# First-layer projections as two 64-row products side by side, and two groups of heads in one attention accumulator

## Chip, core and metric

One core of one Trainium2 chip runs the whole kernel in one launch. The metric is the device time of that core in microseconds (us); lower is better. Engines: PE is TensorE's matrix product and PEld its weight load, DVE is VectorE, ACT is ScalarE, POOL is GpSimd, and SP starts the DMAs.

## What is computed

Two layers work on 16 batches of 512 tokens with 128 features, all in float32. Both have 16 heads of 8 features.

```python
# layer 0, attention (b=16, t=512, H=16, HD=8)
q_c = xh @ W_DQ.T @ W_UQ.T;  q_c_norm = rms_norm(q_c);  q_r = q_c_norm @ W_QR.T
k_c, v_c = split(xh @ W_DKV.T @ W_UKV.T);  k_r = xh @ W_KR.T
scores = concat(q_c_norm, q_r) @ concat(rms_norm(k_c), k_r).T * HD ** -0.5   # causal
out = softmax(scores) @ v_c @ W_O.T
# layer 0, beside it: r * (relu(xk @ W_k.T) ** 2 @ W_v.T), x mixed with the token before
# layer 1, attention: softmax(q @ k.T * scale + phi_bias) @ v, then w_proj and b_proj
# layer 1, beside it: gelu(x @ W1) @ W2, W1 and W2 composed from 32 primitives
```

The weights of layer 0's attention are folded at the start into one matrix `wcat` (128 rows, four blocks of 128 columns: q, k, the second part of k, and the values). As every head uses the same 8x8 map, each block is block-diagonal: it is zero outside its 8x8 blocks, and so also outside the two 64x64 quarters on its diagonal.

## The kernel before

**Bodies and slots.** The work of one batch in one layer is spread over "bodies" of 64 slots, four quarters u = 0 to 3 of 16 slots each. Body n does the attention of batch n (offset 0), prepares batches n+1 and n+2, and finishes batch n-1. In quarter u it computes, for the four heads of group u, the transposed scores (`scores_t`, L643) and, two quarters ahead, the scores once more in the other layout for their row maxima (`scores_max`, L664 and L668, with the causal mask added by products at L680). The two kinds use opposite 64-row halves of the array, so they stand next to each other in the order. ACT exponentiates the transposed scores into `probs` (L937), DVE reduces the maxima (L1144 to L1175), POOL zeroes the causal triangle (`mask`, L1283) or multiplies by the near bias (L1309), and PE multiplies `probs` by the values (`pv`, L627) one quarter later. Each layer has two preparing bodies, sixteen with attention and a finishing one; the last three of layer 0 overlap the first three of layer 1, so 14 attention bodies of layer 0 and 15 of layer 1 run alone.

**Order of the other work.** The tables `WORK_USES` and `OTHER_WORK` (L113 to L129) give for each piece the slot and the batch offset. Each engine walks the slots in order and does what is due (`other`), so an engine that waits for one piece holds back all that stands behind it. The names used below are: OT0 to OT3 (transposes of the accumulator of a group), MT0 to MT3 (transposes of the maxima), XT (transposes of the normalised input), PJ0 to PJ3 (projections of one block of 128 tokens each), QT and KT (queries and keys), FR, FK and FV (the work beside attention), MIX, LN, NORM, SQUARE, MEAN, ROOT and SCALE_QK (steps of DVE and ACT), POST (the two sums of the residual on POOL) and STORE (four indirect DMAs of POOL, L1231).

**PSUM.** Three banks form the ring `scores_transposed`, taken by ACT. Four banks form the ring `scores_for_max`, taken mostly by DVE (`BY_DVE`, L124). A piece claims the next bank of its ring and so waits until the piece three or four claims earlier is read. The eighth bank is `pv_acc`.

**The accumulator.** A group has four heads. Head j of the group writes rows 32j to 32j+31 of `pv_acc`: 8 value sums, the sum of probabilities (a column of ones in `vals`) and 23 rows of zeros. When the four `pv` steps of a group are done, ACT copies the bank to `accS` (L926, at slot 12 of the next quarter), PE transposes it in four products (L693), and DVE takes the reciprocal of the sums (L1045) and multiplies (L1050) into `att`. This is done four times for a batch. In layer 0, POST waits for OT1's result, since it is the last part of `att` of batch n-1.

**The projections.** PJt multiplies 128 tokens (stationary, 128 rows by 128 columns) by the whole of `wcat` (moving, 512 columns), L721, into one bank of `scores_transposed`, and ACT copies it to `big` (L857).

```python
mm(work, xnT[:, B.parity(2), 1 + P * t:1 + P * t + P],
   wcat[:].rearrange("p a n -> p (a n)"), start=True, stop=True)
```

## Time and profile before

| | us |
|---|---|
| median of 3 runs | 1824.24 (1821.36 to 1831.1) |
| the profiled execution's own time | 1823.52 |
| its span, first to last instruction | 1821.7 |
| PE busy | 1622.6 (89%) |
| DVE busy | 1469.0 (81%) |
| ACT busy | 1322.1 (73%) |
| POOL busy | 942.4 (52%) |

The span is the stretch that the trace covers; 1.8 us lie around it. Busy shares are means over stages with different limits. Lines are those of the kernel before. A float32 product is recorded twice (two records of a product and two of its weight load), a float32 transpose once.

### The profile page before, as it was taken

What the parts mean: (1) busy time and instruction counts of PE and PEld (TensorE: products, weight loads), DVE (VectorE), ACT (ScalarE), POOL (GpSimd) and SP (SyncE); (2) the same over time, 40 slices, a digit from 0 to 9 for tenths busy, and PEclk for the clock granted to TensorE, in tenths of its full rate; (3) what the DMA queues carried; (4) which work ended last, traced back from release to release, by engine and by line L of the source; (5) the groups of instructions that cost most, each with busy time, mean ns of one, the idle gap of its engine ahead of it and who ended that gap; (6) DMA issues with size and microseconds to landing.
All of it is one profiled execution on the core that took longest, in us unless ns stands there. A gap on an engine that the chain in (4) does not pass through costs nothing.

```text
span 1821.7 us, 33616 instructions
## 1 busy us (share of the span) xinstructions
PE 1622.6 (89%) x11850; PEld 640.0 (35%) x11850; DVE 1469.0 (81%) x2653; ACT 1322.1 (73%) x2566; POOL 942.4 (52%) x1144
## 2 busy tenths in 40 slices
PE   4798898888889888889999999999999999999995
PEld 2453343333333333333332333323333233333331
DVE  4358878888888788888879888998889888898881
ACT  1227777776777677677778888888888788888875
POOL 2124555555555555455455556655565555564555
PEclk9759999999999999999999999999999999999999
DMA  8312323232322323323222322232222321222200
GB/s 269 58 40 61 68 63 65 62 66 62 71 71 70 67 71 63 71 74 72 59 53 59 59 58 52 46 70 59 58 52 45 71 58 54 48 54 62 61 14 18
DMA packets 133126, 116.41 MB, mean 64 GB/s; under 512 B 16856, under 2 KB 125664, under 8 KB 132960
## 3 DMA queue, kind: packets, MB, share of 16 engines
q1 hardware_dynamic: 126272, 100.64, 24.7%
q0 software_dynamic: 4096, 8.40, 1.4%
q10 hardware_dynamic: 2592, 5.24, 0.9%
q8 instruction: 95, 1.56, 0.4%
q14 instruction: 71, 0.58, 0.1%
HBM read 79.63 MB, written 33.55 MB: 62 GB/s over the span
## 4 chain that ended last, share of the span: by engine, by line
PE 46%; DVE 22%; ACT 10%; issue 7%; POOL 7%; DMA 5%; SPq 2%; DVEq 0%; POOLq 0%; ACTq 0%
PE pv_acc L627 14%; PE scores_transposed L643 10%; ACT probs L937 6%; DVE maxs L1144 4%; PE scores_transposed L771 4%; DMA stacks<-parts_scratch 4%; PE scores_for_max L664 3%; DVE maxs L1147 3%; DVE xn L1067 2%; DVE maxs L1175 2%; POOL x_between_layers L1231 2%; PE scores_transposed L743 2%; PE scores_for_max L779 2%; SPq L478 2%; PE scores_for_max L693 1%
## 5 line engine op out<-in xcount | busy, mean ns | idle before, releaser
L937 ACT ACTIVATE probs<-scores_transposed 128x512 f32<-128x512 f32 x1664 | 919.3, 601 | 214.4 <-PE scores_transposed L643 206.8
L643 PE MATMUL scores_transposed<-stacks 62*128 62x512 bf16 (+3 forms) x2048 | 581.4, 347 | 50.6 <-ACT probs L937 34.4
L1309 POOL TENSOR_TENSOR probs<-probs,near_bias 128x512 f32<-128x512 f32 x256 | 325.1, 1274 | 370.1 <-ACT probs L937 369.8
L627 PE MATMUL pv_acc<-probs,vals 128*32 128x512 f32 (+3 forms) x4096 | 474.8, 536 | 7.8 <-POOL probs L1283 3.8
L1144 DVE TENSOR_REDUCE maxs<-scores_for_max 128x2 f32<-128x1024 f32 x322 | 388.1, 1220 | 78.1 <-PE scores_for_max L664 76.8
L643 PEld LDWEIGHTS scores_transposed<-stacks 62*128 62x128 bf16 x2048 | 153.6, 94 | 618.5 <-ACT probs L937 303.8
L664 PE MATMUL scores_for_max<-stacks 60*128 60x512 bf16 x1024 | 336.3, 385 | 18.1 <-DVE maxs L1144 8.7
L1147 DVE TENSOR_REDUCE maxs<-scores_for_max 128x1 f32<-128x512 f32 x380 | 250.6, 682 | 25.7 <-PE scores_for_max L664 22.6
L668 PE MATMUL scores_for_max<-stacks 60*128 60x512 bf16 (+3 forms) x1024 | 255.1, 315 | 9.8 <-DMA stacks<-parts_scratch 8.0
L1283 POOL TENSOR_SCALAR_AFFINE_SELECT probs<-probs 128x512 f32<-128x512 f32 x256 | 175.4, 700 | 151.1 <-ACT probs L937 150.9
L1175 DVE TENSOR_REDUCE maxs<-scores_for_max 128x1 f32<-128x512 f32 x256 | 174.9, 683 | 90.3 <-PE scores_for_max L680 86.3
L680 PE MATMUL scores_for_max<-causal_halves,ident_halves 64*128 64x128 bf16 (+2 forms) x1280 | 188.6, 235 | 0.0
L1171 DVE TENSOR_REDUCE maxs<-scores_for_max 128x1 f32<-128x384 f32 x256 | 140.3, 548 | 59.0 <-PE scores_for_max L680 58.5
L627 PEld LDWEIGHTS pv_acc<-probs,vals 128*32 128x32 f32 x4096 | 82.4, 109 | 164.8 <-issue 129.3
L680 PEld LDWEIGHTS scores_for_max<-causal_halves,ident_halves 64*128 64x128 bf16 x1280 | 113.8, 99 | 35.8 <-issue 5.7
L1215 POOL TENSOR_TENSOR parts<-rest,parts 128x512 bf16<-128x512 f32 x64 | 75.5, 1180 | 61.0 <-ACT parts L914 61.0
L664 PEld LDWEIGHTS scores_for_max<-stacks 60*128 60x128 bf16 x1024 | 77.0, 93 | 51.2 <-DVE maxs L1144 27.8
L1166 DVE TENSOR_REDUCE maxs<-scores_for_max 128x2 f32<-128x512 f32 x128 | 87.5, 684 | 8.1 <-PE scores_for_max L680 7.0
L693 PE MATMUL scores_for_max<-ident,accS 128*128 128x128 f32 x512 | 85.6, 291 | 1.3 <-ACT accS L926 0.8
L926 ACT ACTIVATE accS<-pv_acc 128x512 f32<-128x512 f32 x128 | 77.3, 604 | 10.4 <-PE pv_acc L627 8.7
L668 PEld LDWEIGHTS scores_for_max<-stacks 60*128 60x128 bf16 x1024 | 76.8, 95 | 21.6 <-DMA stacks<-parts_scratch 8.2
L743 PE MATMUL scores_transposed<-xnT,w 128*128 128x512 f32 x128 | 72.8, 651 | 9.3 <-ACT probs L937 7.9
(129 smaller groups left out, 2093.1 us busy)
## 6 DMA issues: line engine op xcount, KB each, us to landing
stacks<-parts_scratch SPq DMA_DIRECT2D x768, 64.0 KB
parts_scratch<-parts SPq DMA_DIRECT2D x64, 384.0 KB, 2.6
x_tile<-in_L_attn_x_dram SPq DMA_DIRECT2D x16, 256.0 KB, 2.8
probs<-in_fc_B_dram ACTq DMA_DIRECT2D x1, 4096.0 KB, 19.3
stage_a<-in_fc_A_T_dram SPq DMA_DIRECT2D x1, 4096.0 KB, 16.9
stacks<-mT SPq DMA_DIRECT2D x256, 4.0 KB
x_res<-in_L_attn_x_dram SPq DMA_DIRECT2D x16, 256.0 KB, 3.6
x_tile<-x_between_layers SPq DMA_DIRECT2D x16, 256.0 KB
```

Of the source, the lines that this page charges most:

```text
L627: last = mm(acc[32 * j:32 * j + 32, q0:T], vals[:, B.parity(off), kt, G * pu + j, :], probs[:, row, column:column + width], start=(kt == 0 ...
L643: last = mm(st[:, bank, column:column + T - q0], ks[p][rows, h, P * kt:P * kt + P], qs[p][rows, h, q0:T], start=True, stop=True)
L664: mm(bank, qs[p][rows, h, P * qt:P * qt + P], ks[p][rows, h, :], start=True, stop=True).then_inc(s["s1_ready"], 1)
L668: mm(bank[:, column:column + P * (qt + 1)], qs[p][rows, h, P * qt:P * qt + P], ks[p][rows, h, 0:P * (qt + 1)], start=True, stop=False, ski ...
L680: last = mm(masked, ident_halves[half, n, :], mask, start=False, stop=(n == 1), skip_group_check=True)
L937: fn(probs[:, row, :], st[:, B.use(("st", u, number)).bank, :], ACT.Exp, scale=SCALE).then_inc(s["exp_done"], 1)
L1144: v.reduce_max(maxs[:, su % 2, :].rearrange("p (e x) -> p e x", e=E)[:, :, column], s1[:, bank - 1:bank + 1, :], AX_X).then_inc(s["red_don ...
L1147: v.reduce_max(maxs[:, su % 2, column:column + 1], s1[:, bank, :], AX_X).then_inc(s["red_done"], 1)
L1171: v.reduce_max(maxs[:, su % 2, wide:wide + 1], bank[:, 0:3 * P], AX_X)
L1175: v.reduce_max(maxs[:, su % 2, column:column + 1], bank, AX_X).then_inc(s["red_done"], 1)
L1283: g.affine_select(out=diag, in_=diag, compare_op=ALU.is_ge, fill=0.0, base=0, pattern=[[0, G], [1, P]], channel_multiplier=-1).then_inc(s[ ...
L1309: g.tensor_tensor(diag, diag, near_bias[:, kt, :].unsqueeze(1).broadcast_to([P, G, P]), ALU.mult).then_inc(s["emul_pool"], 1)
```

## The change

1. *Accumulator.* Groups 2m and 2m+1 share `pv_acc`: head j of the even group fills rows 32j to 32j+15, head j of the odd group rows 32j+16 to 32j+31. The stationary operand still has 32 columns; for an odd group it begins 16 columns earlier, in the zeros of the head before. The copy to `accS`, the four transposes and the reciprocal are done twice for a batch (OA, OB) and not four times. The reciprocal has 32 columns in place of 16. There are still four multiplications into `att`, now two behind each reciprocal.
2. *Projections.* PJ0 to PJ3 become PJ0 and PJ1. Each claims a bank in both rings and issues four products: for two blocks of tokens, the upper and the lower 64 rows by the 256 columns of `wcat` that are not zero for them. The two halves write different banks, and ACT reads both banks (the names PJ0b and PJ1b stand for the second ones).
3. *Slots.* Layer 0: MIX 0 to 2, FR 5 to 6, FK 8 to 9, XT 11 to 14, MT1 17 to 19, MT2 37 to 32; OT0 (9) and OT2 (40) go, OT1 (16) is OA, OT3 (49) is OB; PJ at 22, 24, 27, 31 becomes PJ at 24 and 31. Layer 1: NORM 16 to 18, OT0 (6) and OT2 (36) go, OT1 (20) is OA (19), OT3 (48) is OB, and AT, PR, VP and STORE move by one slot.

```diff
-VW = 32
+VW, PAIR = 32, 2
+NPAIR = NG // PAIR
+ACC = VW // PAIR
...
 WORK_USES = {
...
+    0: {"MT0": (2, 0, 0), "FR": (6, 0, 1), "FK": (9, 0, 1), "XT": (14, 0, 2), "FV": (15, 0, 1),
+        "OA": (16, 0, -1), "MT1": (19, 0, 0), "PJ0": (24, 0, 2), "PJ1": (31, 0, 2), "MT2": (32, 0, 0),
+        "FT": (35, 0, 1), "QT": (47, 1, 2), "OB": (49, 0, 0), "MT3": (54, 0, 1), "KT": (59, 1, 2)},
+    1: {"H0": (3, 0, 1), "MT0": (4, 0, 0), "H1": (9, 0, 1), "H2": (15, 0, 1), "MT1": (17, 0, 0),
+        "OA": (19, 0, -1), "XT": (21, 0, 2), "AT": (25, 0, -1), "H3": (28, 0, 1), "PR": (30, 0, -1),
...
+BY_DVE = ("OA", "OB", "FV", "QT", "KT", "PR")
+SECOND_HALF = {"PJ0": "PJ0b", "PJ1": "PJ1b"}
...
-    0: {"MIX": (0, 1), "LN": (3, 2), "NORM": (7, 2), "VALUES": (15, 1), "POST": (21, -1),
+    0: {"MIX": (2, 1), "LN": (3, 2), "NORM": (7, 2), "VALUES": (15, 1), "POST": (21, -1),
...
-    1: {"LN": (3, 2), "NORM": (16, 2), "BESIDE": (22, -1), "STORE": (33, -1)},
+    1: {"LN": (3, 2), "NORM": (18, 2), "BESIDE": (22, -1), "STORE": (34, -1)},
...
                     for j in range(G):
...
-                        last = mm(acc[32 * j:32 * j + 32, q0:T], vals[:, B.parity(off), kt, G * pu + j, :],
-                                  probs[:, row, column:column + width], start=(kt == 0), stop=(kt == NT - 1),
-                                  skip_group_check=True)
+                        first = VW * (G * pu + j) - ACC * (pu % PAIR)
+                        last = mm(acc[VW * j:VW * j + VW, q0:T], columns[:, first:first + VW],
+                                  probs[:, row, column:column + width], start=(kt == 0 and pu % PAIR == 0),
+                                  stop=(kt == NT - 1 and pu % PAIR == PAIR - 1), skip_group_check=True)
...
+                        for n, name in enumerate(SECOND_HALF):
+                            if B.due(name, slot):
+                                banks = claim(name), claim(SECOND_HALF[name])
+                                if n == 0:
                                     taken_out("XT")
+                                for t in range(2):
+                                    for e in range(E):
+                                        rows, tokens = slice(HALF * e, HALF * e + HALF), 1 + P * (2 * n + t)
+                                        last = mm(banks[e][:, 2 * P * t:2 * P * t + 2 * P]
+                                                  .rearrange("p (a n) -> p a n", a=4),
+                                                  xnT[rows, B.parity(2), tokens:tokens + P], wcat[rows, :, rows],
+                                                  start=True, stop=True)
+                                        if t == 1:
+                                            last.then_inc(full, 1)
...
+                                for e, half in enumerate((name, SECOND_HALF[name])):
+                                    work = filled(half).rearrange("p (t a n) -> p t a n", t=2, a=4)
...
+                                    fn(big[:, 2 * n:2 * n + 2, :].rearrange("p t (a n) -> p t a n", a=4)
+                                       [:, :, :, HALF * e:HALF * e + HALF], work, ACT.Copy).then_inc(taken, 1)
...
-                            if j == 0 and kt == NT - 1 and B.has(eo):
+                            if j == 0 and kt == NT - 1 and u % PAIR == 0 and B.has(eo):
...
+                            link(v.reciprocal(rsum[:], heads[:, :, HD]), "rec", NPAIR, pair + 1, oo)
...
+                            for n in range(PAIR):
+                                first = G * HD * (PAIR * pair + n)
+                                last = v.tensor_tensor(
...
-                            pool.wait_ge(s["dve_taken"], B.use("OT1").taken[1])
+                            pool.wait_ge(s["dve_taken"], B.use("OA").taken[1])
```

## Rows read from the trace of the kernel before

**Rows 1.** The page, part 1: busy time of each engine.
```profile
PE 1622.6 (89%) x11850; PEld 640.0 (35%) x11850; DVE 1469.0 (81%) x2653; ACT 1322.1 (73%) x2566; POOL 942.4 (52%) x1144
```

**Rows 2.** Windows, three layer-0 periods, slot 32 to 32: length, PE, PEld, DVE, ACT, POOL, clock, DMA.
```profile
487.35:535.82 48.47, 42.87 (x386) 18.71 (x386) 40.06 (x88) 34.76 (x66) 25.94 (x37) 0.96 0.24 67
535.82:583.76 47.94, 42.55 (x386) 18.64 (x386) 39.87 (x88) 34.87 (x66) 26.04 (x37) 0.96 0.25 68
583.76:633.43 49.67, 44.27 (x386) 18.75 (x386) 39.98 (x88) 34.87 (x66) 26.07 (x37) 0.93 0.30 66
```

**Rows 3.** Windows, layer 0: slots 32 to 47, 0 to 15, 16 to 31; next period's 48 to 63.
```profile
487.35:498.65 11.30, 9.37 (x101) 4.43 (x105) 9.61 (x19) 9.84 (x18) 3.72 (x7) 1.00 0.10 26
...
507.70:523.75 16.05, 13.07 (x100) 5.41 (x100) 15.19 (x38) 10.08 (x19) 6.95 (x11) 0.89 0.46 125
523.75:535.82 12.07, 11.87 (x98) 4.76 (x97) 7.93 (x17) 7.98 (x16) 9.12 (x12) 1.00 0.16 45
...
547.04:557.13 10.09, 9.82 (x94) 4.59 (x94) 7.41 (x16) 6.94 (x15) 6.21 (x9) 0.83 0.12 40
```

**Rows 4.** Timeline, start and length, layer 0 around slots 21 to 32, POOL and PE.
```profile
526.60 1.27 POOL L1249 TENSOR_TENSOR x_new<-x_res,att 128x512 f32<-128x512 f32 x1 [1.61 <-DVE att L1050]
...
535.12 0.65 POOL L1283 TENSOR_SCALAR_AFFINE_SELECT probs<-probs 128x512 f32<-128x512 f32 x1
...
535.82 1.06 PE L627 MATMUL pv_acc<-probs,vals 128*32 128x512 f32 x8 [0.21 <-POOL probs L1283]
...
583.76 0.64 PE L627 MATMUL pv_acc<-probs,vals 128*32 128x512 f32 x4 [0.21 <-POOL probs L1283]
```

**Rows 5.** Timeline, layer 0, slots 44 to 47, PE and DVE.
```profile
544.97 0.33 PE L643 MATMUL scores_transposed<-stacks 62*128 62x384 bf16 x1 [1.14 <-ACT probs L937]
544.98 0.33 PE L668 MATMUL scores_for_max<-stacks 60*128 60x384 bf16 x1
...
545.13 1.21 DVE L1096 TENSOR_TENSOR big<-big,rrms 128x1024 f32<-128x1024 f32 x1
...
546.49 0.63 PE L737 MATMUL scores_for_max<-ident,big 128*128 128x128 f32 x4 [0.47 <-DVE big L1096]
```

**Rows 6.** Timeline, layer 0, slots 7 to 11, PE and DVE.
```profile
516.44 0.66 PE L693 MATMUL scores_for_max<-ident,accS 128*128 128x128 f32 x4
...
516.90 2.50 DVE L1067 TENSOR_SCALAR xn<-x_tile,mv,rstd 128x128 f32<-128x128 f32 x4
...
519.55 0.80 PE L704 MATMUL scores_transposed<-ident,xn 128*128 128x128 f32 x4 [1.95 <-DVE xn L1067]
```

**Rows 7.** Groups by form, whole span: count, busy us, mean ns, idle before.
```profile
L721 PE MATMUL scores_transposed<-wcat,xnT 128*128 128x512 f32 x128 | 72.8, 653 | 0.7 <-ACT xnT L839 0.7
L627 PE MATMUL pv_acc<-probs,vals 128*32 128x256 f32 x512 | 41.8, 399 | 0.0
L693 PE MATMUL scores_for_max<-ident,accS 128*128 128x128 f32 x512 | 85.6, 291 | 1.3 <-ACT accS L926 0.8 <-DVE maxs L1147 0.5
L926 ACT ACTIVATE accS<-pv_acc 128x512 f32<-128x512 f32 x128 | 77.3, 604 | 10.4 <-PE pv_acc L627 8.7
L1045 DVE RECIPROCAL rsum<-scores_for_max 128x16 f32<-128x16 f32 x128 | 31.4, 245 | 23.6 <-PE scores_for_max L693 23.6
L1050 DVE TENSOR_TENSOR att<-scores_for_max,rsum 128x128 f32<-128x128 f32 x128 | 37.3, 291 | 4.4
L1092 DVE RECIPROCAL ssq<-ssq 128x128 f32<-128x128 f32 x16 | 15.2, 953 | 0.6
```

**Rows 8.** Windows, one period of layer 1: slots 48 to 63, 0 to 15 and 16 to 31.
```profile
1171.43:1185.23 13.80, 13.80 (x104) 6.24 (x102) 10.94 (x13) 11.73 (x26) 8.60 (x9) 1.00 0.10 31
1185.23:1200.70 15.47, 13.37 (x77) 3.52 (x75) 14.78 (x27) 12.61 (x26) 6.94 (x8) 1.00 0.38 78
1200.70:1215.23 14.53, 13.61 (x88) 4.80 (x87) 12.81 (x19) 12.09 (x24) 7.86 (x8) 1.00 0.44 73
```

**Rows 9.** Timeline, PE: layer 1's slot 15.
```profile
1199.65 1.13 PE L743 MATMUL scores_transposed<-xnT,w 128*128 128x512 f32 x2 [0.61 <-ACT probs L937]
```

More of the change, by code:

```diff
@@ L1036, in other @@
                     u = slot // 16
-                    oo, ou = (-1, u + 2) if u < 2 else (0, u - 2)
-                    if B.out(f"OT{u}", slot):
-                        work = filled(f"OT{u}")
-                        heads = work.rearrange("p (t j c) -> p t j c", t=NT, j=G)
-                        first = Body(layer, B.number - 1).use("OT3") if u == 0 and B.has(-1) else None
-                        before = B.use(f"OT{u - 1}") if u and B.has((-1, -1, -1, 0)[u]) else first
-                        if before:
-                            dve.wait_ge(taken, before.taken[1])
-                        link(v.reciprocal(rsum[:], heads[:, :, :, HD]), "rec", NG, ou + 1, oo)
-                        if ou == 0 and layer == 0 and B.has(oo - 1):
-                            dve.wait_ge(s["post"], B.count(2, 2, oo - 1))
-                        if ou == 0 and layer == 1 and B.number + oo == 0:
-                            dve.wait_ge(S[0]["post"], 2 * NB)
-                        v.tensor_tensor(
-                            att[:, :, G * HD * ou:G * HD * (ou + 1)].rearrange("p t (j d) -> p t j d", j=G),
-                            heads[:, :, :, 0:HD], rsum[:].unsqueeze(3).broadcast_to([P, NT, G, HD]),
-                            ALU.mult).then_inc(taken, 1)
```

77 lines of the change are left out of this document (44 added, 33 removed), and 11 rows, old and new, of the table WORK_USES.

## The prediction

> **What bounds the kernel now.** The page comes first: PE is busy 89% of the span, DVE 81% [rows 1]. Both leave room for a stage in which something else decides, so the next view is the windows of whole periods, one batch from slot 32 to slot 32. In layer 0 a period takes 47.94 to 49.67 us with 42.6 to 44.3 us of PE [rows 2]. Cut into quarters, it shows four different limits [rows 3]: in slots 32 to 47 PE works 9.37 of 11.30 us, DVE 9.61 and ACT 9.84; in slots 0 to 15 DVE works 15.19 of 16.05 and PE 13.07; in slots 16 to 31 PE works 11.87 of 12.07. The last looks like a PE stage, but the timeline tells more. POOL starts POST at 526.60, as soon as DVE has written `att`, and runs without a real pause through two sums, a mask, four indirect DMAs and the mask of group 1, which ends at 535.77. PE's first `pv` of group 1, at slot 32, starts 0.05 us later and had waited 0.21 us for it; one period on, the same 0.21 us [rows 4]. So two chains of equal length end at slot 32: PE's, and POOL's of 9.2 us from `att`.
>
> The clock must be read beside this. A period with a granted clock of 0.96 takes 48.47 or 47.94 us, one with 0.93 takes 49.67 [rows 2]. The clock is 0.89 in slots 0 to 15 and 1.00 in the neighbouring quarters [rows 3]: a short stretch at 1.2 GHz in place of 2.4. PE stood idle for 1.95 us ahead of XT just before [rows 6]. The other place is slot 48, behind the idle 1.14 and 0.47 us of [rows 5]; the period from 535.82 on has its lowered stretch there (0.83 from 547.04 on [rows 3]). Against the period with both, one without the stretch after XT is 1.73 us shorter (49.67 - 47.94), one without the stretch after slot 48 is 1.20 us shorter (49.67 - 48.47).
>
> In layer 1 the clock is 1.00. PE fills slots 48 to 63 (13.80 of 13.80); in slots 0 to 15 DVE works 14.78 of 15.47 and PE 13.37 [rows 8].
>
> **Projections.** Before: 128 records, so 64 products, in 72.8 us [rows 7], 1.14 us each, 4.55 for a batch. After: 4 pairs of products of 64 rows and 256 columns. That two halves of the array run side by side is seen in bfloat16: two products of 0.33 us start 0.01 us apart [rows 5]. For float32 of 256 columns the nearest row is `pv`, four products side by side: 512 records, 64 sets, 41.8 us, so 0.65 us for a set [rows 7]. I take 4 x 0.65 = 2.6 us, which frees 2.0 us of PE. Bounds: eight in sequence, 5.2 us (0.65 us more), and half of before, 2.3 us (2.3 us less). All of it lies in slots 16 to 31, ahead of the mask that PE already waits for [rows 4]. PE will come to slot 32 some 2 us earlier and wait some 2.4 us there. Worth on the path: 0. If POOL's chain were shorter, the whole 2.0 us would count. ACT's four copies keep their size and lie under the same wait; the second bank that a projection claims is freed by ACT, and a late one hides there too.
>
> The halved product might leave its readers as the limit. ACT works 7.98 us in slots 16 to 31 [rows 3], below the 9.9 us that PE keeps, so the copies do not bind; POOL does. The Trainium skill, page "TensorEngine Tiling (Array Packing)", section "PSUM Bottleneck", says that tiling speeds up the products but not the reading of PSUM, whose copy may become the limit. The trace does not agree for this stage. By that rule the stage would keep the 2.0 us; by the rows it keeps none.
>
> **What the clock makes of that wait.** An idle PE of 1.95 us is followed by a lowered clock [rows 3, 6]; one of 2.4 us should be too. The first `pv` (1.06 us) and the scores behind it, on which ACT and DVE wait, would be late. Bounds: 0 and 1.73 us for a batch, the price after XT [rows 2]. Part of the lowered stretch falls on the wait itself or on slots with slack, so I take 0.8 us.
>
> **Accumulator, layer 0.** Each set of four transposes costs 85.6/128 = 0.67 us of PE, each copy 0.60 us of ACT, each reciprocal and multiplication 0.245 + 0.291 = 0.54 us of DVE [rows 7]. OT0 (slot 9) stands in the quarter that DVE binds: -0.54 us. OA, ahead of POST, is longer: a second multiplication of 0.29 us, and 32 columns in the reciprocal. Between 16 columns (245 ns) and 128 (953 ns) it is 6.3 ns a column, so +0.10 us. Together +0.39 us, on POOL's chain. OT2 (slot 40) stood on DVE ahead of SCALE_QK (L1096), for which QT waited 0.47 us [rows 5]: -0.4 us. The copies at slots 28 and 60 and the other transposes lie beside longer work. The `pv` products keep count and width: 0. OB's +0.39 us of DVE falls on slots 49 and up, where PE leads: 0, and up to 0.39 if DVE were late there.
>
> **Moved steps, layer 0.** XT waits for NORM on DVE, 2.50 us long and behind MIX and LN [rows 6]. At slot 14 XT itself waits less, but PE cannot pass DVE by more than the four banks of the maxima, so most of the 1.95 us comes back as a wait for a bank at slot 14, about 1.7 us. The lowered clock there, in two of the three periods, becomes a little rarer: -0.3 us (bounds 0 and 1.73). MIX, FR and FK move by two or one slots, still behind LN's and NORM's place: 0 to +0.4, taken as 0. MT2 earlier puts its SP transfer earlier, no queue behind it suffers.
>
> Layer 0 for a batch: -0.54 + 0.39 - 0.4 + 0.8 - 0.3 = -0.05 us, times 14 bodies that run alone: -0.7 us.
>
> **Layer 1.** OT2 (slot 36) stands ahead of PE's full stretch: -0.6 us. OT0 (slot 6) stands where DVE binds, up to slot 22: -0.54 us of DVE, +0.39 for OA at 19, so -0.15. The two copies, 0.60 us each, relieve ACT, for which PE waits 0.61 us at slot 15 [rows 9]: between 0 and -0.6, taken as -0.15, since they stand elsewhere. NORM two slots later still leaves XT at 21 several slots; were it late, that is the loss of a rival below. Sum -0.9 us, bounds -0.3 and -1.8; times 16: -14.4 us. In the last batch OT0 stands ahead of the last `pv` with nothing beside it: -0.6 + 0.39 = -0.2 us. The start and the three shared bodies are taken as 0.
>
> **Sum.** -0.7 - 14.4 - 0.2 = -15.3 us on the profiled execution's 1823.5 us: 1808.2. The median of the runs is 0.7 us above that execution: 1809 us. A measurement of this kernel tells 0.5% (9 us) from no change.
>
> **Rivals.**
> *The clock stays up.* The wait at slot 32 costs no clock and the one at slot 14 is short enough. Layer 0: -0.54 + 0.39 - 0.4 - 1.15 (1.73 in two of three) = -1.7 us, x14 = -24: 1785 us. For: one period of three had no lowered stretch after its wait for XT. Against: 2.4 us is longer than 1.95. Chance 0.17.
> *The projections count.* POOL's chain is not what holds slot 32: -0.54 + 0.39 - 0.4 - 2.0 - 0.3 = -2.85 us, x14 = -40: 1769 us. Against: the same wait in both rows of [rows 4]. Chance 0.10. This is where the page's rule of "PSUM Bottleneck" would lead, too.
> *The halves do not overlap.* The change does not do what it says; PE needs 0.65 us more, comes to slot 32 about 0.4 us late, and the clock stays up: layer 0 about -0.5 us, x14 = -7: 1802 us. Against: the pairs in bfloat16. Chance 0.06.
> *Layer 1 gives nothing.* NORM at 18 and OA at 19 stand together ahead of the reductions of slots 20 to 23, and PE waits there for banks: -0.2 us, x16 = -3: 1820 us. Chance 0.10.
> *Slower: the wait at slot 32.* PE idles long enough in every batch, and the lowered clock falls wholly on the first `pv` and scores of group 1: +1.73 us; DVE's -0.54 and +0.39 stay, and QT gains nothing as ACT is late: +1.6 us, x14 = +22; with layer 1 at its weaker bound of -5: 1841 us. It decides from a loss in layer 0 of 1.0 us a batch if layer 1 gives 0.3, or 1.7 if it gives 0.9. For: slots 32 to 47 have ACT at 9.84 and DVE at 9.61 of 11.30, little to absorb a late start. Chance 0.13.
>
> **Numbers.** The forecast, 1809 (own range 1798 to 1821), has 0.44. Faster by over 0.5%: the first three rivals (0.33) and most of the forecast (0.35), 0.68. Within 0.5%: the rest of the forecast and the fourth rival, 0.19. Slower: 0.13. The range, 1770 to 1834, leaves out about half of the rival at 1769 and most of the slower one.
>
> **What would show it.** Right: PE waits about 2.4 us for the mask at slot 32 in layer 0, POOL's 9.2 us unchanged; projections of about 0.65 us a pair; the clock lowered behind slot 32; QT without its wait; a layer-0 period near 48.5 us and one of layer 1 shorter by about 0.9. Wrong: a period of layer 0 under 47 us or over 50 us, no wait at slot 32, or a layer-1 period that has not moved.

## The result and the profile after

The median of 14 runs is 1842.01 us (1829.75 to 1850.58), against 1825.64 us (1821.36 to 1831.1) in 14 runs of the kernel before on the same chip: a ratio of 1.0094, 95% interval 1.0078 to 1.011. The change makes the kernel slower by 0.9%, where faster was forecast; 1842 also lies above the range. Ratios here leave out runs over 1.5% above the fastest of the same kernel (one each of e2, at 2659.74 us, of e4 and of e16, and five of the twelve of e10), medians do not.

The page of the kernel after, parts 1 and 2, answers to [rows 1]:

```profile
PE 1602.5 (87%) x11722; PEld 633.7 (34%) x11722; DVE 1446.7 (78%) x2571; ACT 1286.2 (70%) x2502; POOL 927.0 (50%) x1144
...
PEclk9759888889888888899889999999999999999998
```

Every engine works less than before, PE by 20 us, DVE by 22, ACT by 36, and the span is 25.8 us longer (1847.5 against 1821.7). PEclk has many 8s in the first half, which is layer 0. Windows of twelve whole periods of layer 0 and of layer 1 (length, PE, PEld, DVE, ACT, POOL, clock, DMA share, GB/s), first of after, then of before:

```profile
198.70:814.12 615.42, 518.63 (x4633) 232.54 (x4633) 471.27 (x1032) 408.98 (x756) 297.52 (x445) 0.87 0.25 63
1081.39:1757.83 676.44, 632.51 (x4030) 210.83 (x4029) 594.27 (x864) 552.21 (x1117) 388.31 (x407) 0.98 0.25 57
```

```profile
193.86:780.57 586.71, 518.49 (x4632) 224.78 (x4632) 479.83 (x1057) 419.96 (x781) 312.71 (x444) 0.96 0.29 66
1042.89:1730.46 687.57, 646.23 (x4126) 223.09 (x4125) 604.14 (x906) 568.47 (x1140) 386.94 (x407) 1.00 0.25 56
```

A period of layer 0 went from 586.71/12 = 48.89 to 51.29 us (+2.40), one of layer 1 from 57.30 to 56.37 (-0.93). Twelve of each make +28.7 and -11.1; the start lost 4.8 us (198.70 against 193.86), the bodies between the two windows 5.0 (267.3 against 262.3), and the end won 1.6: together +25.8. In layer 0 PE's busy time is the same to 0.1 us, although there is less for it to do; the clock of 0.87 in place of 0.96 used up what was saved. After was profiled in an execution of 1849.37 us, 7 above its median, and before in one of 1823.52, so the windows show some 25 us of difference where the medians show 16.

One period of after by quarters (slots 32 to 47, 48 to 63, 0 to 15, 16 to 31), against [rows 3]:

```profile
557.49:570.55 13.06, 10.94 (x93) 4.81 (x93) 9.52 (x17) 9.50 (x16) 3.22 (x7) 0.76 0.08 23
570.55:580.41 9.86, 9.81 (x94) 4.50 (x93) 7.05 (x17) 7.00 (x15) 5.91 (x9) 0.84 0.10 32
580.41:595.53 15.12, 12.08 (x100) 4.69 (x96) 14.43 (x36) 9.81 (x19) 6.36 (x11) 0.96 0.48 98
595.53:608.87 13.34, 10.49 (x107) 5.30 (x106) 8.10 (x18) 7.71 (x15) 9.28 (x13) 0.88 0.43 86
```

As means over twelve periods, from one start of a group's `pv` to the next, the quarters changed by +1.61 (11.37 to 12.98), +0.13 (9.57 to 9.70), -0.35 (15.62 to 15.27) and +1.02 us (12.33 to 13.35). Where PE waits in that period, with POOL's work ahead of the first wait (timeline: start, length, idle before and its releaser):

```profile
548.25 1.27 POOL L1269 TENSOR_TENSOR x_new<-x_res,att 128x512 f32<-128x512 f32 x1 [2.76 <-DVE att L1068]
...
555.82 0.96 POOL L1251 DMA_INDIRECT x_between_layers<-x_new,slots_now  x1 [0.30 <-issue]
556.79 0.65 POOL L1303 TENSOR_SCALAR_AFFINE_SELECT probs<-probs 128x512 f32<-128x512 f32 x1
```

```profile
553.61 0.48 PE L731 MATMUL scores_transposed<-wcat,xnT 64*128 64x256 f32 x1
...
554.37 0.38 PE L731 MATMUL scores_for_max<-wcat,xnT 64*128 64x256 f32 x1
557.49 1.93 PE L634 MATMUL pv_acc<-probs,vals 128*32 128x512 f32 x8 [2.75 <-POOL probs L1303]
559.36 0.60 PE L650 MATMUL scores_transposed<-stacks 62*128 62x512 bf16 x1
...
568.90 0.33 PE L650 MATMUL scores_transposed<-stacks 62*128 62x384 bf16 x1 [2.12 <-ACT probs L954]
...
592.67 0.33 PE L675 MATMUL scores_for_max<-stacks 60*128 60x384 bf16 x1 [1.52 <-DVE maxs L1192]
```

POOL's chain from POST to the end of the mask (557.44) is 9.19 us, as before. PE is done with PJ1 at 554.74 and waits 2.75 us at slot 32; the first `pv` of group 1 then takes 1.93 us in place of 1.06. Two more waits stand at slots 44 to 47 (2.12, before 1.14 and 0.47 [rows 5]) and at slot 14 (1.52). A fourth, of 1.07 us early in slots 0 to 15, stands in before too (1.02), and no lowered clock begins behind it in either. The granted clock behind the wait at slot 32, in after and then in before:

```profile
557.49:563.51 6.02, 6.02 (x35) 2.23 (x35) 2.96 (x4) 3.24 (x6) 2.07 (x5) 0.50 0.07 19
```

```profile
535.82:541.80 5.98, 5.66 (x58) 2.28 (x59) 4.33 (x7) 4.91 (x10) 2.19 (x5) 1.00 0.02 5
```

For 6.02 us PE runs at 1.2 GHz without a pause, and what stands behind it gets 35 records of products in place of 58. Over the twelve periods the clock records show 13.3 us at 1.2 GHz a period (before: 4.3). These lowered stretches begin behind the wait at slot 14 in 12 of 12 periods, around slot 32 in 10 (there 0.4 to 1.6 us ahead of the end of the wait), and behind slots 44 to 47 in 11; before, behind the wait for XT in 10 of 12, never around slot 32, and behind slots 44 to 47 in 5.

### The profile page after: what moved, and what is told of

It is laid out like the page before. It is cut to its first block, busy times and chain, and to the rows that moved or that the text cites. A ratio compares the mean times of both kernels' runs of the same rounds, so it can differ in the third digit from the quotient of the medians.

```text
span 1847.5 us, 32996 instructions
## 1 busy us (share of the span) xinstructions
PE 1602.5 (87%) x11722; PEld 633.7 (34%) x11722; DVE 1446.7 (78%) x2571; ACT 1286.2 (70%) x2502; POOL 927.0 (50%) x1144
## 4 chain that ended last, share of the span: by engine, by line
PE 54%; DVE 21%; ACT 10%; issue 6%; POOL 5%; DMA 2%; SPq 1%; DVEq 0%; POOLq 0%; ACTq 0%
PE pv_acc L634 17%; PE scores_transposed L650 12%; ACT probs L954 5%; PE scores_transposed L785 4%; PE scores_for_max L671 3%; DVE maxs L1164 3%; DVE xn L1087 2%; POOL x_between_layers L1251 2%; PE scores_transposed L757 2%; DVE maxs L1191 2%; DVE maxs L1195 2%; PE scores_for_max L793 2%; PE scores_for_max L675 2%; DMA stacks<-parts_scratch 2%; PE scores_for_max L687 2%
## 5 line engine op out<-in xcount | busy, mean ns | idle before, releaser
L954 ACT ACTIVATE probs<-scores_transposed 128x512 f32<-128x512 f32 x1664 | 907.8, 602 | 265.2 <-PE scores_transposed L650 256.7
L634 PE MATMUL pv_acc<-probs,vals 128*32 128x512 f32 (+3 forms) x4096 | 507.9, 570 | 44.2 <-POOL probs L1303 36.0
L1164 DVE TENSOR_REDUCE maxs<-scores_for_max 128x2 f32<-128x1024 f32 x340 | 409.2, 1220 | 76.1 <-PE scores_for_max L671 74.1
L671 PE MATMUL scores_for_max<-stacks 60*128 60x512 bf16 x1024 | 327.2, 388 | 12.3 <-DVE maxs L1164 8.6
L675 PE MATMUL scores_for_max<-stacks 60*128 60x512 bf16 (+3 forms) x1024 | 263.1, 323 | 34.3 <-DVE maxs L1192 22.7
L1195 DVE TENSOR_REDUCE maxs<-scores_for_max 128x1 f32<-128x512 f32 x256 | 175.0, 683 | 148.1 <-PE scores_for_max L687 147.6
L1303 POOL TENSOR_SCALAR_AFFINE_SELECT probs<-probs 128x512 f32<-128x512 f32 x256 | 161.9, 647 | 177.5 <-ACT probs L954 177.3
L1167 DVE TENSOR_REDUCE maxs<-scores_for_max 128x1 f32<-128x512 f32 x344 | 226.3, 683 | 25.5 <-PE scores_for_max L671 23.2
L687 PE MATMUL scores_for_max<-causal_halves,ident_halves 64*128 64x128 bf16 (+2 forms) x1280 | 196.9, 240 | 0.0
L1260 POOL TENSOR_TENSOR rstd<-mv,minus_half 128x4 f32<-128x4 f32 x32 | 40.2, 1257 | 71.4 <-DVE mv L1083 71.4
L1251 POOL DMA_INDIRECT out_dram<-x_new,slots_now x64 | 63.0, 984 | 24.7 <-issue 14.8
```

What stands on the lines that cost most here:

```text
L634: last = mm(acc[VW * j:VW * j + VW, q0:T], columns[:, first:first + VW], probs[:, row, column:column + width], start=(kt == 0 and pu % PAI ...
L671: mm(bank, qs[p][rows, h, P * qt:P * qt + P], ks[p][rows, h, :], start=True, stop=True).then_inc(s["s1_ready"], 1)
L675: mm(bank[:, column:column + P * (qt + 1)], qs[p][rows, h, P * qt:P * qt + P], ks[p][rows, h, 0:P * (qt + 1)], start=True, stop=False, ski ...
L687: last = mm(masked, ident_halves[half, n, :], mask, start=False, stop=(n == 1), skip_group_check=True)
L954: fn(probs[:, row, :], st[:, B.use(("st", u, number)).bank, :], ACT.Exp, scale=SCALE).then_inc(s["exp_done"], 1)
L1164: v.reduce_max(maxs[:, su % 2, :].rearrange("p (e x) -> p e x", e=E)[:, :, column], s1[:, bank - 1:bank + 1, :], AX_X).then_inc(s["red_don ...
```

## The experiments

Eighteen kernels ran, in groups beside the kernel before on the same chip (medians of before: 1824.2 for e1 to e4, 1824.6 for e5 to e8, 1820.3 for e9 to e12, 1822.5 for e13 to e16, 1827.5 for e17 and e18, so a difference of medians across groups is good to some 7 us). Medians in us; "clock" and the two periods are of windows of twelve periods, as above; "lowered" is the time at 1.2 GHz in a layer-0 period, from the clock records. Clock, lowered and periods are of one profiled execution each; those of e4 and e7 took 12 us more than their median, those of after and e13 7 and that of e8 5 more, those of e2, e5 and e18 7, 9 and 5 less.

| | median | ratio, interval | layer 0 | clock | lowered | layer 1 |
|---|---|---|---|---|---|---|
| before | 1825.64 | | 48.89 | 0.96 | 4.3 | 57.30 |
| after | 1842.01 | 1.0094 (1.0078 to 1.011) | 51.29 | 0.87 | 13.3 | 56.37 |
| e1 after, old products | 1820.92 | 0.9984 (0.9963 to 1.0005) | 49.23 | 0.94 | 6.3 | 56.30 |
| e2 before, new products | 1814.97 | 0.9955 (0.9932 to 0.9978) | 47.85 | 0.96 | 3.4 | 57.17 |
| e3 after, products twice | 1820.35 | 0.9979 (0.9956 to 1.0002) | 48.79 | 0.94 | 5.4 | 56.90 |
| e4 after, spread store | 1795.62 | 0.9819 (0.978 to 0.9857) | 47.71 | 0.90 | 9.1 | 56.62 |
| e5 after, old slots | 1839.45 | 1.0092 (1.0061 to 1.0123) | 50.33 | 0.90 | 10.0 | 56.27 |
| e6 e2 + spread store | 1793.95 | 0.9831 (0.9793 to 0.987) | 47.47 | 0.93 | 6.5 | 56.81 |
| e7 e4 + old slots | 1782.62 | 0.9761 (0.9728 to 0.9794) | 46.44 | 0.94 | 5.7 | 56.88 |
| e8 e4 + FK twice | 1758.14 | 0.9646 (0.961 to 0.9682) | 44.88 | 0.96 | 4.0 | 56.56 |
| e9 after, FK twice | 1794.57 | 0.9862 (0.9826 to 0.9897) | 47.76 | 0.92 | 7.7 | 56.47 |
| e10 accumulator alone | 1833.09 | 1.0016 (0.998 to 1.0053) | 49.79 | 0.91 | 9.1 | 56.78 |
| e11 before, spread store | 1818.74 | 0.9988 (0.9968 to 1.0007) | 48.68 | 0.96 | 4.3 | 57.04 |
| e12 before, FK twice | 1812.0 | 0.9948 (0.9927 to 0.9968) | 47.86 | 0.98 | 1.7 | 56.95 |
| e13 after, square moved | 1834.79 | 1.0074 (1.0055 to 1.0094) | 50.66 | 0.88 | 11.8 | 56.28 |
| e14 e4 + square moved | 1795.04 | 0.9856 (0.9833 to 0.9878) | 47.79 | 0.89 | 10.2 | 56.58 |
| e15 before, square moved | 1822.77 | 1.0006 (0.9986 to 1.0025) | 48.69 | 0.96 | 4.3 | 56.94 |
| e16 e14 + FK twice | 1766.37 | 0.9675 (0.9642 to 0.9709) | 45.48 | 0.95 | 4.6 | 56.42 |
| e17 after, square waits | 1803.11 | 0.9877 (0.9847 to 0.9907) | 48.02 | 0.92 | 7.7 | 56.35 |
| e18 e4 + square waits | 1761.15 | 0.965 (0.9611 to 0.9689) | 44.36 | 0.96 | 4.0 | 56.58 |

### The parts, one by one

**e1: the change without its products.** PJ0 to PJ3 at slots 22, 24, 27 and 31, as before; the accumulator and all moved slots stay.

```diff
-mm(banks[e][...], xnT[rows, B.parity(2), tokens:tokens + P], wcat[rows, :, rows], ...)
+mm(work, xnT[:, B.parity(2), 1 + P * t:1 + P * t + P], wcat[:].rearrange("p a n -> p (a n)"), ...)
```

> The changed kernel with the four products of 128 rows by 512 columns back at slots 22, 24, 27 and 31; accumulator and all other slots as changed. Theory A (the freed PE time turns into a wait of 2.7 us for POOL at slot 32 of layer 0, and the clock falls behind it): PE needs about 2 us more per batch in slots 16 to 31, the wait shrinks to 0.2 to 0.5 us, the clock stays up there, the layer-0 period falls from 51.4 to about 48 us, and the time to 1805 to 1818 us, although PE works more. Theory B (the pairing of groups or the moved slots made layer 0 slower, not the products): the layer-0 period stays above 50.5 us and the time at 1835 us or more.

1820.92 us, 3 above the range of theory A: with 2.3 us more of PE work a batch it is 21 us faster than after. PE's idle time ahead of slot 32 is 0.75 us in the mean (after 2.88), and no lowered stretch begins there. The loss goes with the products, though not by them alone, as the next runs show.

**e2: the products alone**, in the kernel before.

```diff
-"PJ0": (22, 0, 2), "PJ1": (24, 0, 2), "PJ2": (27, 0, 2), "PJ3": (31, 0, 2)
+"PJ0": (24, 0, 2), "PJ1": (31, 0, 2)
...
```

The products and their two banks are those of the change.

> The kernel before with the projections alone changed (two banks, pairs of 64 rows, slots 24 and 31); accumulator and other slots as before. Theory A: layer 0 loses as much as in the full change or more (period 50.5 to 52 us in place of 48.6), layer 1 keeps its period of 57.6, so 1850 to 1875 us, slower than the full change. Theory B: no loss from the products, 1815 to 1828 us.

1814.97 us, faster than before, where theory A had expected 1850 and more. The same wait stands at slot 32. Windows and timeline of e2:

```profile
526.96:531.20 4.24, 4.24 (x30) 2.06 (x34) 2.28 (x4) 3.54 (x7) 2.08 (x5) 0.60 0.01 4
531.25:574.41 43.16, 36.19 (x368) 17.41 (x361) 37.70 (x85) 31.44 (x60) 23.41 (x33) 1.00 0.32 75
```

```profile
479.34 1.30 PE L629 MATMUL pv_acc<-probs,vals 128*32 128x512 f32 x8 [2.55 <-POOL probs L1294]
```

The clock falls behind slot 32 here too (in 8 of 12 periods), but a period has hardly another such stretch: behind the wait for XT one begins in 4 of 12 periods (before: 10), behind slots 44 to 47 none (before: 5). So the wait at slot 32 alone doesn't make the change slow; that reading fell.

**e10: the accumulator alone**: e1 with MIX, FR, FK and XT at their old slots too.

> The kernel before with the paired accumulator alone: old products, MIX, FR, FK and XT at their old slots. It completes the square of before (layer-0 period 48.9), new products alone (47.9) and both (51.3, or 50.3 at old slots). Theory I (the two parts hurt each other, through waits that add up until the clock falls everywhere): accumulator alone 48.3 to 49.3 us, layer 1 0.9 us shorter per batch, 1805 to 1816 us. Theory II (the accumulator alone costs layer 0 its 1.4 us and more): 50 us or more, 1825 us or more.

Median 1833.09, 13 us above before's in the same group (1820.3). Eleven of its twelve runs took 1826 to 1841 us and one 1806; the ratio of 1.0016 (0.998 to 1.0053) rests on the seven fastest. So there is no gain, and by the medians a loss of 0.7%, though DVE and ACT have less to do and layer 1 keeps -0.52 us a period; theory II (1825 and more) is the nearer one. In layer 0 two waits of PE are longer than in before, for ACT at slots 44 to 47 (before 1.14) and for XT (before 1.95):

```profile
654.74 0.33 PE L647 MATMUL scores_transposed<-stacks 62*128 62x384 bf16 x1 [1.74 <-ACT probs L942]
...
677.11 0.63 PE L708 MATMUL scores_transposed<-ident,xn 128*128 128x128 f32 x4 [2.55 <-DVE xn L1075]
```

Each is 0.6 us longer, about the 0.67 us of the four transposes (OT2 at slot 40, OT0 at 9) that PE no longer has ahead of it: this part of the change, too, turned PE's work into waits. Lowered stretches begin behind the first in 9 of 12 periods (before 5) and at the second in 11 (before 10), 9.1 us a period in place of 4.3. Windows of e10 show two kinds of period in one execution:

```profile
542.79:594.05 51.26, 44.75 (x378) 19.38 (x378) 39.45 (x86) 34.28 (x63) 25.45 (x38) 0.87 0.29 63
645.59:693.75 48.16, 41.41 (x378) 17.89 (x378) 39.49 (x86) 34.09 (x63) 25.35 (x38) 0.96 0.33 67
```

The instructions and the two waits (1.74 and 2.54 to 2.55 us) are the same, and the length differs by 3.1 us, with the clock.

**e5: after with the old slots** of MIX, FR, FK and XT.

```diff
-"FR": (6, 0, 1), "FK": (9, 0, 1), "XT": (14, 0, 2)   "MIX": (2, 1)
+"FR": (5, 0, 1), "FK": (8, 0, 1), "XT": (11, 0, 2)   "MIX": (0, 1)
```

> The changed kernel with MIX, FR, FK and XT of layer 0 back at slots 0, 5, 8 and 11. In the changed kernel the clock is lowered three times in nearly every layer-0 period: behind a wait of 1.5 us for a bank at slots 12 to 15, behind the one of 2.9 us at slot 32 and behind the one of 2.0 us at slots 44 to 47; in the kernel with new products alone, which has the old slots, the first is missing in 11 of 12 periods although PE waits 1.9 us for XT. Theory S (the moved slots brought the first lowered stretch): the layer-0 period falls from 51.3 to 49 us or less, the time to 1800 to 1818 us. Theory A (the wait at slot 32 alone decides, wherever XT stands): 50.5 us and more, 1832 us and more.

1839.45 us: with both parts in, the moved slots make no difference (with the old products they gain 12 us, e1 against e10, and with the spread store they cost 13, e4 against e7). The expectation is wrong in one point: in e2 the first stretch is missing in 8 of 12 periods, not 11. By the ratios the products alone gain 0.45% (e2), and both parts together at the same slots lose 0.92%. The layer-0 period changes by -1.0 us with the products, by +0.9 with the accumulator (e10) and by +1.4 with both: the parts do not add up.

### The clock or the work

**e3: each projection's product issued twice** into the same bank, so that PE has 8 products more and the result doesn't change.

```diff
+                                for t in range(2):
+                                    for e in range(E):
+                                        mm(banks[e][...], ..., start=True, stop=True)
```

> The changed kernel with each of the eight projection products issued twice into the same place, so that PE has about 2 us more work per batch of layer 0 in slots 24 and 31 and nothing else changes. Theory A (wait and clock): the extra work fills the wait at slot 32 and keeps the clock up: the kernel gets FASTER with more work, 1808 to 1825 us. If the wait alone cost time and not the clock, the time would stay within 4 us of the changed kernel's 1842. Theory C (the new products themselves, their two rings or the tiling are what costs): 16 times 2 us more, 1865 to 1885 us.

1820.35 us: more work for PE, 22 us less time. PE's idle time ahead of slot 32 falls from 2.88 to 1.13 us, and no lowered stretch begins between slots 28 and 43 (after: 10 of 12 periods). The lowered clock falls from 13.3 to 5.4 us a period. Work in the place of waiting wins nothing by itself, so what the wait costs, it costs through the clock.

**e4: layer 0's store spread out.** The four indirect DMAs stand at slots 26, 33, 37 and 41 and not all at 26.

```diff
+STORE_AT = (26, 33, 37, 41)
...
-                    for t in range(NT):
+                    for t in range(NT if layer else 0):
                         store_rows(t)
+                    if layer == 0 and B.has(-1) and slot in STORE_AT:
+                        store_rows(STORE_AT.index(slot))
```

> The changed kernel with layer 0's four indirect DMAs of POOL apart, at slots 26, 33, 37 and 41, in place of all four at slot 26; same DMAs, same sizes. POOL's chain from att to the mask of group 1 is then some 3.8 us shorter. Theory A: the wait at slot 32 goes, the projections' 2 us count, the layer-0 period falls from 51.4 to 45.5 to 47.5 us, the time to 1765 to 1795 us, faster than both kernels. If the masks of slots 36 to 47 become late behind the moved DMAs, the gain is about half, 1800 to 1815 us. Theory B or C: no more than 5 us from the changed kernel's 1842.

1795.62 us, 46 less than after. Windows of e4, slots 32 to 47 and 16 to 31, and its `pv` at slot 32:

```profile
478.45:489.99 11.54, 9.49 (x95) 4.79 (x93) 9.80 (x18) 11.08 (x19) 7.15 (x10) 0.89 0.14 43
...
515.40:526.23 10.83, 10.70 (x107) 5.45 (x106) 8.07 (x18) 6.55 (x13) 5.61 (x8) 0.87 0.06 19
```

```profile
478.45 1.07 PE L635 MATMUL pv_acc<-probs,vals 128*32 128x512 f32 x8
```

The `pv` has no wait and takes 1.07 us, and slots 16 to 31 are 2.5 us shorter than in the period of after: PE now fills them (10.70 of 10.83). **e11**, the same in the kernel before, and **e6**, e2 with it, tell whose gain this is.

> The kernel before with the store spread alone. In it PE and POOL arrive at slot 32 together (wait 0.24 us), so spreading the store alone should give 0.2 us per batch: 1818 to 1826 us. If POOL held more than the trace shows: under 1812 us.

> The kernel before with the new products and with layer 0's four indirect DMAs apart (slots 26, 33, 37, 41); accumulator and other slots as before. With the store spread POOL no longer holds slot 32, and the new products' 2 us should count: the layer-0 period falls from 47.9 (new products alone) to 45.5 to 46.5 us, the time to 1785 to 1800 us. If POOL's chain was not what held it: 1810 to 1820 us as with the products alone.

e11: 1818.74 us, no difference that can be told; there PE's own work ends at slot 32 as late as POOL's. e6: 1793.95 us, 21 less than e2, though its layer-0 period is 47.5 us and not the 45.5 to 46.5 expected. The new products bring 25 us where POOL's chain has been shortened (e6 against e11) and 9 where it has not (e2); a shorter chain of POOL brings 21 us where PE's work has been cut, and 2 where it has not.

### Slots 12 to 15

e4 still has 9.1 us of lowered clock a period, 12 of 12 behind slot 14. **e7**, e4 with the old slots (the edit of e5), moves the place:

> The changed kernel with the store spread and with MIX, FR, FK and XT of layer 0 at their old slots. Theory S: also here the lowered clock at slots 12 to 15 becomes rarer, and the time falls from the 1796 us of the spread store to 1770 to 1785 us, the best of all. Otherwise 1790 to 1805 us.

1782.62 us, 13 less than e4. **e8, e9 and e12** issue the product of FK twice into the same bank, as a filler of 1.0 us shortly ahead of that wait; e8 in e4, e9 in after, e12 in before.

```diff
                                 mm(work, wrkv[:, n, :], (fa, fb)[n][:], start=True, stop=True).then_inc(full, 1)
+                                # ahead of it, where n is 1: the same product without then_inc
```

> The changed kernel with the store spread, and the product FK of layer 0 (128x512, 1.06 us of PE) issued twice into the same bank. PE then comes 1.06 us later to slots 12 to 15, where it waits 0.45 and 1.51 us in every period for POOL and DVE. Theory (it is the clock that costs there, not the wait): the waits fall below 1 us together, the clock stays up at slot 12, and the time falls from 1796 us to 1775 to 1790 us in spite of 16 us more products. If only PE's work counts: 1796 to 1813 us.

> The changed kernel (store together at slot 26) with the product FK of layer 0 issued twice. Theory (the clock, wait by wait): the waits of 0.45 and 1.51 us at slots 8 to 15 shrink by 1.06 us together and lose their lowered stretch; those at slots 28 to 31 (2.9 us) and 44 to 47 (2.0 us) and their stretches stay. One stretch fewer of three at 1.2 to 1.7 us each: layer-0 period 51.3 to 49.0 to 50.0 us, 1805 to 1824 us. If only work counts: 1842 to 1859 us.

> The kernel before with FK issued twice. PE's wait for XT, 1.92 us at slots 8 to 11, falls to about 0.9 us and loses its lowered stretch (4.3 us of lowered clock per period, two thirds of it there): the layer-0 period falls from 48.9 to 47.0 to 48.0 us, 1800 to 1816 us, with 16 us more of products. If only work counts: 1825 to 1841 us.

1758.14, 1794.57 and 1812.0 us: 37, 47 and 8 us less than the same kernels without it (for e12, than before in its own group). In e8 and e9 that is more than the theory had expected, by 17 and 10 us. It looks as if a filler kept the clock up. But in e8 and e9 a second thing changed (not in e12, where NORM still takes 2.47 us). DVE's NORM and POOL beside it, in after and then in e9 (timeline; then the view of NORM's line over twelve periods: shortest, median and longest piece in ns, first and last start):

```profile
538.02 0.62 POOL L1303 TENSOR_SCALAR_AFFINE_SELECT probs<-probs 128x512 f32<-128x512 f32 x1
538.07 2.50 DVE L1087 TENSOR_SCALAR xn<-x_tile,mv,rstd 128x128 f32<-128x128 f32 x4
538.62 1.03 POOL L1264 TENSOR_TENSOR fd<-fd 128x512 f32<-128x512 f32 x1
539.61 0.62 POOL L1303 TENSOR_SCALAR_AFFINE_SELECT probs<-probs 128x512 f32<-128x512 f32 x1
```

```profile
L1087 DVE TENSOR_SCALAR xn<-x_tile,mv,rstd x48: 331/661/1095, 230.8 to 796.9; 128x128 f32<-128x128 f32 x48
```

```profile
505.38 0.62 POOL L1305 TENSOR_SCALAR_AFFINE_SELECT probs<-probs 128x512 f32<-128x512 f32 x1
505.44 1.42 DVE L1089 TENSOR_SCALAR xn<-x_tile,mv,rstd 128x128 f32<-128x128 f32 x4
506.69 1.06 POOL L1266 TENSOR_TENSOR fd<-fd 128x512 f32<-128x512 f32 x1 [0.69 <-ACT fd L867]
```

```profile
L1089 DVE TENSOR_SCALAR xn<-x_tile,mv,rstd x48: 332/335/664, 218.6 to 745.4; 128x128 f32<-128x128 f32 x48
```

In after POOL works without a gap beside NORM (538.02 to 540.23), and NORM takes 2.50 us. In e9 the late product makes POOL's square late, POOL pauses, and NORM takes 1.42. Two theories remained: N, NORM beside POOL's work makes DVE late, PE waits for it, and the clock falls; F, the filler keeps the clock up.

**e13, e14, e15** move the square from slot 10 (before: 9) to 12: in after, in e4 and in before (there with 4 in place of the 3 below). **e16** is e14 with FK twice.

```diff
-                        if B.out("FK", slot, 1):
+                        if B.out("FK", slot, 3):
```

> The changed kernel; POOL squares the product FK (fd) at slot 12, behind the mask of that slot, and not at slot 10; nothing is repeated or left out. In the runs with FK issued twice, NORM on DVE took 415 ns a piece in place of 685, because POOL squared 1.1 us later and no longer beside it. Theory N (NORM beside POOL's work is what costs): NORM near 415 ns a piece, the wait of 1.5 us at slots 12 to 15 and the lowered clock behind it go, a layer-0 period near 47.8 us and a time near 1795 us, without any repeated product. Theory F (the repeated product keeps the clock up): nothing is repeated, so 1842 us stay, within 6.

> The changed kernel with layer 0's four indirect DMAs spread over slots 26, 33, 37, 41, and the square of FK at slot 12; nothing is repeated. Theory N: near 1758 us, the time of the version with spread stores and FK twice, or some us less as 1.1 us of PE a batch is saved. Theory F: 1796 us stay.

> The kernel before; POOL's square of FK at slot 12 and not 9. Theory N: NORM near 415 ns, XT's wait 1.95 us goes to about 0.9, a layer-0 period 48.9 to about 47.8, some 1808 us. Theory F: the gain of FK twice here (1812 us, NORM unchanged at 677 ns) came from the repeated product, so 1824 us stay within 5, or XT's wait shortens and the time doesn't.

> The spread stores, the square of FK at slot 12, and FK issued twice. Theory N: NORM is short in either case, so the repeated product brings nothing, and costs its 1.1 us of PE where PE leads: 0 to +15 us on the run without it. Theory F: it brings a gain of 30 us and more on the run without it.

1834.79, 1795.04, 1822.77 and 1766.37 us. For N the first three tell nothing, since NORM stayed at 686 ns a piece: in the place of the square the mask of slot 12 came forward. e16 does tell: with NORM as long as in e14 (687 ns), the repeated product brings 29 us. So F holds for as much as that, just short of the 30 it had asked for, and e12 agrees. **e17 and e18** test N by itself, in after and in e4:

```diff
                         if B.out("FK", slot, 1):
+                            if B.has(2):
+                                pool.wait_ge(s["xn_done"], B.count(NT, NT, 2))
```

> The changed kernel; POOL waits for the end of NORM (xn_done) ahead of its square of FK, so that only the first mask stands beside NORM. Nothing is repeated or left out. Moving the square by itself (e13) only brought the next mask beside NORM, and NORM stayed at 686 ns a piece; this run keeps all of POOL's later work away from it. Theory N: NORM near 415 ns, the wait of 1.5 us at slots 12 to 15 near 0.5, its lowered clock gone, some 1800 us. Theory F (the repeated product is what brings the time): NORM short as well, but the time within 15 us of 1842.

> The same with the spread stores. It completes a square: neither 1795 us (1796 and 1795), the repeated product with NORM long 1766, both 1758. Theory N: about 1760 us. Theory F: 1780 to 1790 us, as a shorter NORM brings only the 8 us that stand between 1766 and 1758, or up to its 1.08 us in 14 batches, 15 us.

1803.11 and 1761.15 us, where N had said some 1800 and about 1760, and F within 15 us of 1842 and 1780 to 1790. NORM takes 413 and 414 ns a piece; its 1.08 us in 14 batches make 15 us, and 39 and 34 were won. Timelines of POOL and PE in e17, and its quarters (slots 32 to 47, 48 to 63, 0 to 15, 16 to 31):

```profile
511.50 0.62 POOL L1305 TENSOR_SCALAR_AFFINE_SELECT probs<-probs 128x512 f32<-128x512 f32 x1
513.06 1.04 POOL L1266 TENSOR_TENSOR fd<-fd 128x512 f32<-128x512 f32 x1 [0.94 <-DVE xn L1087]
```

```profile
480.75 1.07 PE L634 MATMUL pv_acc<-probs,vals 128*32 128x512 f32 x8 [2.75 <-issue]
490.95 0.33 PE L650 MATMUL scores_transposed<-stacks 62*128 62x384 bf16 x1 [2.12 <-ACT probs L954]
...
513.70 0.33 PE L675 MATMUL scores_for_max<-stacks 60*128 60x384 bf16 x1 [0.44 <-DVE maxs L1192]
```

```profile
480.75:492.64 11.89, 9.77 (x93) 4.74 (x94) 9.56 (x17) 9.48 (x16) 3.26 (x7) 0.84 0.09 25
492.64:502.51 9.87, 9.82 (x94) 4.44 (x93) 7.02 (x17) 6.97 (x15) 5.88 (x9) 0.84 0.10 32
502.51:515.93 13.42, 11.46 (x99) 4.68 (x95) 13.28 (x36) 9.49 (x19) 6.16 (x9) 1.00 0.47 116
515.93:528.32 12.39, 9.52 (x106) 5.24 (x105) 8.23 (x20) 8.07 (x16) 9.54 (x14) 1.00 0.39 86
```

The wait at slot 14 is 0.44 us in place of 1.52, and a lowered stretch begins there in 1 of 12 periods, not 12. Against the period of after above, slots 0 to 15 are 1.70 us shorter, slots 16 to 31 0.95 us, and both have a clock of 1.00. The wait at slot 32 is as long as in after (2.75 us), and the clock falls there too, but in most periods only 0.4 to 1.6 us behind the end of the wait, and for less: the `pv` takes 1.07 us, and slots 32 to 47 take 11.89 us at 0.84 in place of 13.06 at 0.76.

The four kernels with the spread store: NORM long and no filler 1795 (e4 1796, e14 1795), filler only 1766, NORM short only 1761, both 1758. Either does nearly all, and the second adds 3 to 8 us, about the scatter between groups. Both work on the same thing, the wait at slot 14 with the lowered clock behind it in every period (e16: a wait of 1.19 us in the mean, the clock in 5 of 12; e18: the clock in none).

## Why the prediction was wrong

**Held.** *Projections.* PE needs 554.74 - 553.61 = 1.13 us for two pairs, so 2.3 us a batch against 4.55: the forecast was 2.6, and 2.3 was its lower bound. *Worth on the path: 0, for POOL's chain holds slot 32.* The wait came (2.75 us, forecast some 2.4) and POOL's 9.2 us are unchanged; e6 against e2 and e11 shows that most of the time counts only once that chain is shortened. The Trainium skill, page "TensorEngine Tiling (Array Packing)", section "PSUM Bottleneck", says that the copies from PSUM may become the limit; ACT works 7.71 of 13.34 us in that quarter, and e4, which doesn't touch the copies, gives 46 us. *Accumulator:* the reciprocal of 32 columns takes 348 ns (forecast 345), and QT's wait is gone; but the 0.4 us given for that are not won, as the wait just ahead of it grew. *Layer 1:* -0.93 us a period, forecast -0.9; its three terms were not measured apart, and the clock there went from 1.00 to 0.98. *Bank wait at slot 14:* 1.52 us, forecast about 1.7.

**The steps that failed** are the two that price the clock, both in layer 0. *"What the clock makes of that wait"* took +0.8 us of bounds 0 to 1.73. The quarter behind slot 32 lost 1.61 us, near the upper bound; the sum had taken "part falls on the wait itself or on slots with slack", but [rows 3] had ACT at 9.84 and DVE at 9.61 of 11.30 us there, as the prediction's slower rival says. *"Moved steps, layer 0"* took -0.3 us for a rarer lowered clock. It became more frequent (12 of 12 against 10), and, what the step did not see at all, it moved: with the wait at slot 14 and not ahead of XT at 11, it lies across the start of slot 16 and delays what DVE and PE do ahead of POST, where POOL's 9.2 us begin. Slots 16 to 31 lost 1.02 us, of which 0.39 had been forecast for OA; in e17, without that lowered stretch, they are 0.87 us shorter again. Slots 0 to 15 won 0.35 us, where the accumulator and the rarer clock had been given 0.54 and 0.3.

The prediction also put nothing on what the accumulator's own cut does to PE. The wait at slots 44 to 47 grew from 1.14 to 2.12 us and is followed by a third lowered stretch in 11 of 12 periods (before 5). Of that growth 0.6 us comes with the accumulator (e10: 1.74), next to none with the products alone (e2: 1.19 in the mean), and the last 0.3 only with both. The terms of layer 0 in place of -0.05: +1.61 + 0.13 - 0.35 + 1.02 = +2.4 us. "The start and the three shared bodies are taken as 0" failed as well: they lost 4.8 and 5.0 us, and no run takes them apart. A small slip of the sum: layer 1 was counted sixteen times, and fifteen of its bodies run alone, 0.9 us.

The rival "Slower: the wait at slot 32", 1841 us with a chance of 0.13, gave the right time partly by luck: it had +1.6 us a batch and a gain in layer 1 of 5 us; it was +2.4, with 11 us won in layer 1. Its mechanism is half of the truth. By e2 the wait at slot 32 alone is no loss against before, by e17 it stands unchanged in a kernel 39 us faster than after. What is slow is three waits in one period, each with the lowered clock behind it in most periods.

**The cause.** Freed time on PE turned into waits: for POOL at slot 32, for DVE at slot 14, for ACT at slots 44 to 47. Two of them can each be taken away by itself, the first by spreading the store (-46 us, e4), the second by keeping POOL off NORM (-39 us, e17), and the two effects about add up (-81 us, e18). With the lowered clock as rare as in before (4.0 us a period), e18 is 0.965 of before, 3.5% faster (interval 0.9611 to 0.9689), and e8 is level with it (0.9646); e18 repeats nothing and is the version to keep. How much of the 3.5% is the change's and how much would come from the two edits of POOL alone is not shown, since before ran only with the spread store (e11, no difference). In e18 the lowered clock stands behind slots 44 to 47 in 9 of 12 periods, and in one behind a wait for a DMA that after and e17 do not have:

```profile
368.55 0.39 PE L651 MATMUL scores_transposed<-stacks 62*128 62x512 bf16 x1 [3.79 <-DMA stacks<-mT]
```

Such a wait stands behind slot 32 in 3 of 12 periods of e18 (1.19 to 3.79 us) and in 3 of e8 (3.63 to 4.28 us, each with a lowered stretch). What makes that transfer late was not tried.

**Open:** why the clock falls behind the same wait at once in one kernel and later in another (slot 32 in after and e17), and longer in one period than in the next behind equal waits (e10), so also why the products alone (e2) do without the other two stretches. The idle time of PE in a period doesn't tell: before has 5.7 us of it, e2 7.3 and after 8.1, and e2 has less lowered clock than before. Not tried: a version of before with the square behind NORM, and one with the waits at slots 44 to 47 shortened.

## What to carry to other kernels

Ahead of a cut in PE's work, ask what ends at the same point by another chain: if one does, the cut becomes a wait, and a wait can cost more than the work did (here 22 us less time with the work put back, e3), so price it at its upper bound where the engines behind it have no slack. Shorten the other chain in the same change; here that is POOL's, by spreading its DMA issues. And where an instruction takes longer than its twins elsewhere, look at what the neighbouring engine does in that moment before you take its duration as given.
